# A scan's GpSimd order: decayed x ahead of a later head's mask, and head 0's first tap and decay ahead of head 1's weight parts

## What is computed

```python
def _L1_attn_ref(x, in_proj_w, conv_w, conv_b, dt_bias, A_log, D, norm_w, out_proj_w):
    H, P, N, G, K, CH, E = (32, 128, 128, 8, 4, 32, 256)
    proj = x @ in_proj_w.T
    gate, hbc, dt = jnp.split(proj, [I, I + CD], axis=-1)
    ...                                    # causal convolution, 4 taps, then silu
    hs, B, C = jnp.split(hbc, [I, I + G * N], axis=-1)
    dt = jax.nn.softplus(dt.astype(jnp.float32) + dt_bias)
    X = hs.reshape(b, s, H, P) * dt[..., None]
    ...                                    # A_cum: running sums of A*dt in a chunk
    Y_diag = jnp.einsum('bclhn,bcshn,bhcls,bcshd->bclhd', Cc, Bc, Lmat, Xc)
    states = jnp.einsum('bclhn,bhcl,bclhd->bchdn', Bc, decay_states, Xc)
    new_states = jnp.einsum('bhij,bjhdn->bihdn', decay_chunk, states)
    Y_off = jnp.einsum('bclhn,bchdn,bhcl->bclhd', Cc, states_prev, state_decay)
    y = (Y_diag + Y_off).reshape(b, s, H, P) + D_res
    h32 = y * jax.nn.silu(gate)
    ...                                    # RMS norm over groups of 512, norm_w
    return norm_w * h32 @ out_proj_w.T
```

## Time and profile before

| | us |
|---|---|
| median of 3 runs | 1625.67 |
| lowest and highest run | 1623.1, 1629.16 |
| profiled execution | 1630.07 |
| its span in the trace | 1628.3 |
| TensorE matmul busy in the span | 1423.7 (87%) |
| VectorE busy | 1139.8 (70%) |
| ScalarE busy | 878.0 (54%) |
| GpSimd busy | 496.3 (30%) |

### The profile page before, as it was taken

How to read it: one execution, slowest core, us unless ns; L and a number is a source line. 1 busy time by engine, 2 the same in 40 slices (tenths; PEclk the granted TensorE clock), 3 DMA queues, 4 the chain that set the end, 5 groups by cost and what they waited for, 6 DMA issues and landing times. The chain is left out here.

```text
span 1628.3 us, 25033 instructions
## 1 busy us (share of the span) xinstructions
PE 1423.7 (87%) x7896; PEld 1052.3 (65%) x7896; DVE 1139.8 (70%) x2026; ACT 878.0 (54%) x1238; POOL 496.3 (30%) x407
## 2 busy tenths in 40 slices
PE   2999489999999965997697987899999999999697
PEld 2788333333333335886585876788888888888586
DVE  6532599998989946522675684887878778778475
ACT  2422227776767744421433775767666666765432
POOL 1444110000000021543100013565657566565200
PEclk7999759999999976999798898999999999999899
DMA  8533211111111009323201002322222223231200
GB/s 294 155 53 46 59 32 16 25 25 25 28 26 27 8 10 363 54 47 60 82 1 34 26 23 85 97 79 98 78 98 91 84 90 97 78 97 53 78 1 26
DMA packets 83020, 111.92 MB, mean 69 GB/s; under 512 B 11904, under 2 KB 60800, under 8 KB 82912
## 3 DMA queue, kind: packets, MB, share of 16 engines
q1 hardware_dynamic: 73152, 96.05, 19.6%
q0 software_dynamic: 9376, 14.16, 4.9%
q10 hardware_dynamic: 384, 0.39, 0.1%
HBM read 89.99 MB, written 11.93 MB: 63 GB/s over the span
## 5 line engine op out<-in xcount | busy, mean ns | idle before, releaser
L962 DVE TENSOR_REDUCE attn_max_chunks<-attn_scores 128x1 f32<-128x512 f32 x488 | 305.1, 683 | 31.9 <-PE attn_scores L1213 26.5
L1124 ACT ACTIVATE attn_probs<-attn_scoresT 128x1024 f32<-128x1024 f32 x256 | 248.2, 1022 | 121.0 <-PE attn_scoresT L1229 120.8
L1213 PE MATMUL attn_scores<-attn_k_picks,attn_q_group 64*128 64x512 f32 x488 | 189.4, 468 | 14.3 <-DVE attn_max_chunks L962 6.0
L1213 PEld LDWEIGHTS attn_scores<-attn_k_picks,attn_q_group 64*128 64x128 f32 x488 | 86.1, 192 | 178.3 <-DVE attn_max_chunks L962 170.4
L1644 DVE SCALAR_TENSOR_TENSOR ssm_scan_x<-ssm_scan_proj,ssm_w_conv,ssm_scan_x 128x1023 f32<-128x1023 f32 (+2 forms) x96 | 123.0, 1282 | 56.9 <-ACT ssm_scan_x L1639 51.2
L1229 PE MATMUL attn_scoresT<-attn_q_group,attn_k_picks 64*128 64x512 f32 x512 | 155.2, 441 | 3.2 <-ACT attn_probs L1124 3.2
L1241 PE MATMUL attn_o<-attn_probs,attn_v_group 128*32 128x512 f32 x1024 | 139.7, 618 | 0.4 <-ACT attn_probs L1124 0.3
L62 PE MATMUL ssm_scan_proj<-ssm_xnT_hi,ssm_w_in_hi 128*128 128x512 f32 x256 | 110.6, 432 | 18.1 <-DVE ssm_scan_x L1644 16.1
L293 POOL DMA_INDIRECT moe_sums<-moe_xn,moe_token x46 | 78.2, 1699 | 128.9 <-DVE moe_xn L430 118.6
L1639 ACT ACTIVATE ssm_scan_x<-ssm_scan_proj,ssm_b_conv,ssm_w_conv 128x1024 f32<-128x1024 f32 x32 | 38.5, 1205 | 138.6 <-DVE ssm_scan_v L2268 135.5
L481 ACT ACTIVATE moe_xnT<-moe_gate 128x512 f32<-128x512 f32 x46 | 27.5, 598 | 154.2 <-PE moe_gate L64 154.2
(11 more groups left out here) (361 smaller groups left out, 3403.2 us busy)
## 6 DMA issues: line engine op xcount, KB each, us to landing
ssm_cum_all<-ssm_cums SPq DMA_DIRECT2D x32, 512.0 KB, 3.8
ssm_scan_exp_cum<-ssm_cums SPq DMA_DIRECT2D x32, 512.0 KB, 3.7
moe_w_gate_lo<-in_moe_w SPq DMA_DIRECT2D x16, 512.0 KB, 11.2
moe_w_up_lo<-in_moe_w SPq DMA_DIRECT2D x16, 512.0 KB, 11.1
moe_w_down<-in_moe_w SPq DMA_DIRECT2D x16, 512.0 KB, 11.3
ssm_w_in<-in_in_w SPq DMA_DIRECT2D x64, 128.0 KB, 2.5
ssm_scan_w_out<-in_out_w SPq DMA_DIRECT2D x7, 512.0 KB, 3.8
moe_sums<-main_residual SPq DMA_DIRECT2D x2, 1024.0 KB, 5.6
```

Source lines behind the costliest of these rows:

```text
L962: return nc.vector.tensor_reduce(rmaxc[:, half, place:place + 1], chunk_bank(g, n), AX_X, ALU.max).then_inc(reduced, 1)
L1124: nc.scalar.activation(probs[s % 2][:, 2 * pair:2 * pair + 2, :], st_ps[pair][:], ACT.Exp, scale=SCALE).then_inc(exp_done, 1)
L1213: nc.tensor.matmul(chunk_bank(g, n), qs[b][head_rows(j), t * P:(t + 1) * P], kz[b][head_rows(j), j % 2, c * BANK:(c + 1) * BANK], start=Tr ...
```

## The change

Three orders are changed; no instruction is added or taken away, and no shape or buffer changes.

- In each head's `body` on GpSimd, `xend_of(n + 1)` now stands ahead of `mask_later(n + 2)`.
- For head 0 on GpSimd, `low(1, 1)` stands behind `cgrow_of(0, 0)` instead of ahead of all, and `xend_of(0)` ahead of `mask_later(1)`.
- On ScalarE, `high(1, 1)` is no longer the first instruction: `ahead` now calls it for head 0 as for the others, behind the first tap, the exp and the decay.

```diff
@@ gpsimd, body
                     cgrow_of(n + 1, (j + 1) % G)
+                    xend_of(n + 1)
                     if not is_at(n, LAST - 1):
                         mask_later(n + 2)
-                    xend_of(n + 1)
                 sum_squares(n, j, gw)
 
-            low(1, 1)
             pool.wait_ge(q["consts"], 2)
             mask_later(0)
             cgrow_of(0, 0)
+            low(1, 1)
+            xend_of(0)
             mask_later(1)
-            xend_of(0)
             heads(pool, body)
@@ scalar, ahead
-                if after(n, 1) and not is_at(n, LAST):
+                if not is_at(n, LAST):
                     high(n + 1, 1 - j % 2)
...
-            high(1, 1)
             act.wait_ge(q["consts"], 2)
```

## The result

| | before | after |
|---|---|---|
| median, us | 1627.41 (6 runs, 1623.1 to 1634.94) | 1611.63 (6 runs, 1605.95 to 1617.67) |
| profiled execution, us | 1630.07 | 1611.65 |
| span, us | 1628.3 | 1609.9 |

The ratio is 0.9893, with a 95% interval of 0.9867 to 0.9919: 1.1% faster, and 1611.63 stands beside a forecast of 1610.6.

A forecast was written before the change was run, and what follows sets the result against it. Bounds: the loop through gated in loop heads and heads 1-3, TensorE in unrolled heads, TensorE after its xend wait in scaled heads. 6.36 + 1.50 + 2.88 + 2.85 + 1.46 = 15.05 us off 1625.67 gives 1610.6 us; range 1604 to 1618.

The forecast's parts named there:

- These two terms: Unrolled heads: TensorE's wait goes, 8 x 0.36 = 2.88 us; loop heads and heads 1-3: gated 0.19 us earlier, 2.85 us.
- Rival 1: Both xend halves get ahead of gated; 15 heads lose 12.0 us of the sum: 1622.6 us; chance 0.09.
- Rival 4: GpSimd keeps the port through halves, `landed` and mask before gated: slower, 1640 us; chance 0.02.
- Rival 2: Gated precedes xend's first half in loop heads too; 12 heads gain 0.4 us more: 1605.8 us; chance 0.10.
- The term of the scaled heads: Heads 8, 12, ... 28: xend's first half starts 1.06 us earlier and all arrives, 6 x 1.06 = 6.36 us.
- Head 4: First head with scaled output weights: its wait for xend goes altogether, 1.50 us.
- The start: Head 0: without the weight cast in front, ScalarE's first tap starts 1.46 us earlier and the rest follows.
- a bound for the gate projection: Gate projection at the start ran at half clock; full clock would save 2.6 us more; taken as 0, range only.
- the sum of 15.05: Total saving forecast, us: 6.36 + 1.50 + 2.88 + 2.85 + 1.46, giving 1610.6 us, 0.93% less.
- The cover of the mask: Moved mask ends 2.9 us ahead of its reader, ScalarE's decay; squares start later, so moving it costs nothing.
- Rival 3: Scaled heads' long waits give way to others of the same size, 6.36 us don't arrive: 1617.0 us; chance 0.07.
- Rival 5: Reorder does nothing, xend waits for VectorE's scaled x; only the start stays: 1624.2 us; chance 0.03.

The follow-up runs named there:

- experiment 5: Kernel after, with GpSimd also waiting for the gated product (gated) before xend in every head; 1607.79 us, ratio 0.987.
- experiment 10: Kernel after with all 32 heads written out, no hardware loop; 1601.33 us, ratio 0.9835.
- experiment 3: Kernel before with GpSimd's new order only in the scaled heads (4, 8, ... 28); 1620.12 us, ratio 0.9946.
- experiment 1: Kernel before with GpSimd's new order in the body alone, start as before; 1612.86 us, ratio 0.9907.
- experiment 8: Kernel after run and profiled once more, unchanged; 1615.31 us, ratio 0.9911 against the kernel before.
- experiment 2: Kernel after with the body's old order put back, so only the start is new; 1626.47 us, ratio 0.9983.
- experiment 12: Kernel before with all 32 heads written out, no hardware loop; 1623.84 us, ratio 0.9969.
- experiment 4: Kernel after with the mask and `landed` made twice per head behind xend; 1619.51 us, ratio 0.9942.
- experiment 9: Kernel after with GpSimd waiting for gated before xend only in unscaled heads except the last; 1600.58 us, ratio 0.9826.
- experiment 6: Kernel after with the scaling of the output weights behind xend instead of ahead of cgrow; 1611.57 us, ratio 0.9881.
- experiment 7: Kernel after with both the wait for gated before every xend and the weight scaling behind xend; 1610.02 us, ratio 0.9885.

## Why the prediction came out right

**The mechanism held where it was read from rows.** Gated ends 2.09 us after cgrow (2.08 forecast), in all unscaled heads; turn-taking between the halves, seen once ahead of the change, in head 31, is the rule. The written-out heads go to 14.75, the loop heads to 15.14. These two terms gave 2.9 and 2.2 us in 20 heads, 2.88 and 2.28 forecast. That gated binds the loop heads, by VectorE's longer chain there, is shown by experiments 5 and 10. Rivals 1 and 4 are refuted by the 2.09. Rival 2 did not come by itself, but experiment 5 shows that its price was right: with gated ahead of the halves the loop heads lose 0.37 us each, 0.4 in the rival.

**The term of the scaled heads was too small.** It took the mask's 1.06 us as the gain. Measured is 1.20: xend's first half ended 2.11 us behind gated before (1191.29 + 1.05 against 1190.23) and ends 0.90 behind it now. The missing 0.14 is what lay around the mask: `landed`'s end, and a first half that now follows gated at once. Gated's end to xend's, less a half, would have given it. Head 4 gave 1.76 for 1.50; experiment 3 puts 1.26 of it on the head itself. Head 24 gave 1.46. In experiment 3, with the new order in the scaled heads alone, it took 17.50, and 17.23 to 17.25 wherever the unscaled heads have the new order as well (experiments 1 and 8). There gated becomes ready only after cgrow's end (1371.28 against 1370.97), so xend's first half runs ahead of it and TensorE no longer waits. Head 28 gave 2.06, but 0.53 of that is not the order's: in experiment 2, with the body's old order, it took 18.57 and not 19.10. Why those two differ by that stays open; without the loop (experiments 12 and 10) it gave 1.3.

**The start was worth 3.85, not 1.46.** The order itself gave 1.40, nearly as forecast. The clock gave 2.45 more, and the text had put it at nothing, with 2.6 as a bound for the gate projection. That projection gave only 0.86 of it, since it still ran 3.4 us at half clock. The other 1.59 came from head 1's gate projection, which the text did not name. So the bound held in size, but not for the reason given, and taking 0 was the wrong choice. The start repeats: 25.2 to 25.3 us in six profiles with the new start, 29.0 to 29.4 in three with the old, and from the end of head 0's gate projection to `from_states` 12.3 us in those six against 13.9 in those three. Where the first projection itself meets half clock (four profiles with the new start, 26.9 to 27.5 us; experiment 1 with the old, 27.3, one profile) the new order gains nothing, since the cast is then hidden behind the slower projection. What decides that lies ahead of the scan, and the runs don't show it.

**The loop's turn was not in the sum.** TensorE's stall and the half clock behind it take 5.5 us (22.99 against 17.50 in head 12). The prediction looked for what is late next among engines and transfers of data, and not at the fetching of instructions, which the queue's packets point to. Against the sum of 15.05 the scan gave 2.4 more at the start, 0.3 in head 4 and 1.9 in heads 8, 12, 20, 24 and 28 (7.2 for 5.3), and 5.35 less at head 16 (4.29 lost for 1.06 gained): 14.2. That they nearly cancel is luck: without the loop's turn the same change is worth 20.96 us in the scan (experiments 12 and 10).

**The cover of the mask was sized at the wrong reader.** The text gave it 2.9 us, up to the decay, and called the squares later than that. Experiment 4 shows that in the scaled heads the squares come right behind the mask with 0.86 us to spare. For this change it made no difference, since nothing was added behind xend.

**Rivals 3 and 5** are refuted by experiment 3: only scaled heads in the new order, and their 1.20 us arrive.

## What to carry to other kernels

Between two engines that exclude each other by whole instructions, count what one of them has to sit through at each place of an order, and break a long block of the one where the other's short instruction is on the path; if the turns don't fall that way, one wait (1.22 against 1.84 us for gated, experiments 5 and 9) makes them, but only put it where the other would not have gone first anyway. When work is moved back, its cover is the time to the first reader of anything behind it in the queue, not to its own reader. And after a change to code in a hardware loop look at the first instructions of its second turn: 5 us can lie there that no data dependence shows.

## What the runs showed of the hardware

**The second turn of a hardware loop may cost TensorE 3.6 to 4.3 us of stall, or nothing.** With the loop, eight of eleven profiles have it, with 61 packets on the instruction queue each time. The kernel before and experiments 4 and 5 don't, with 52. This is the queue over 154 us, from 22 us before the last `from_states` of the first turn to 1 to 2 us behind the last one of the second, in the new kernel and then in the kernel before:

```profile
q8 instruction: 9, 0.15, 0.4%
```

```profile
q8 instruction: 1, 0.02, 0.0%
```

So in the one something is fetched all through the second turn, in packets of 1.00 / 61 = 0.0164 MB by the whole queue, which I read as the loop's code. In the other there is none of it: its one packet comes ahead of the turn. The Trainium skill (Runtime: NRT & Kernel Launch, "Instruction fetch mechanics") says that TensorE has room for 128 KiB of instructions in blocks of 16 KiB. The 16.4 KB a packet agree with it. The same section of the Trainium skill says that a taken branch whose target isn't in the current window of two pages stalls for a DMA. The stall agrees with that in eight profiles. In the other three the loop branches back without a fetch or a stall, over code that takes 9 packets where it is fetched, so a window of two pages does not describe them. An estimate from the 128 KiB of the Trainium skill: 9 blocks are about as much as the 8 of the room, so that little would decide; no run here shows what does. The change and experiments 1 to 9 leave TensorE's own instructions as they are, so the time at which blocks are asked for may be it. That is argued, not shown. Writing the loop out ends it (experiment 10).

**Half clock follows short idleness, but not each time.** In experiment 4 idle times of 0.58 and 0.34 us in one head are followed by 3.8 us at 1.2 GHz (0.55 granted); in the new kernel 0.58 us alone in the same head is not, and its projection runs at full clock. There 0.60 us of delay cost 2.18.
